# Attention in three passes, with maxima and exponentials of one pass side by side, scores by parts of the keys, and two row transfers in flight

## Chip, cores and metric

The kernel runs on one core of one Trainium2 chip, in one launch. The metric is the device time of the execution in microseconds (us); lower is better. A core has TensorE (PE; its weight loads are shown as PEld), VectorE (DVE), ScalarE (ACT), GpSimd (POOL) and SyncE (SP), which run side by side and wait for each other by semaphores. TensorE writes to PSUM, which has eight banks of 512 fp32 values per partition; SBUF is the working memory.

## What is computed

Two layers over 2048 tokens of width 128. Layer 0 is an attention block and a mixture of experts (eight experts, the two best per token); layer 1 is a recurrence over the tokens and a second mixture (one expert per token). The change lies in the attention of layer 0 and in the first sending of its tokens to the experts. The attention works on the first tokens only, in three iterations, and each may widen its window `cw` by a tenth:

```
def step(carry, i):
    qcur, prev, attn, cw, temp, done = carry
    ...
    scores = jnp.einsum('bhqd,bhkd->bhqk', sq, sk) * inv_sqrt_e
    in_win = pos < cw
    scores = jnp.where(in_win[None, None, None, :], scores, -jnp.inf)
    probs = jax.nn.softmax(scores, axis=-1)
    out = jnp.einsum('bhqk,bhkd->bhqd', probs, vp)
    iter_out = jnp.where(in_win[None, None, :, None], out, 0.0)
    diff = jnp.mean(jnp.abs(iter_out - prev))
```

There are 16 heads of width 8. The largest possible windows of the three iterations are 256, 281 and 309 keys (`WINDOWS`), so 2, 3 and 3 tiles of 128 tokens. These first three tiles of 128 tokens are the "near" tokens; the other 13 are the "far" tokens, which attention doesn't change.

## The kernel before

The program is written engine by engine, by hand: each engine runs its instructions in the order written, and semaphores join them.

**A pass of attention** (`attend(it)` on PE and on DVE, `softmax_exp(it)` on ACT; the text calls the iterations pass 0, 1 and 2). Queries and keys are split into bf16 pieces that are laid side by side in `stack`, 64 values a head, turned by TensorE (L1004, "turn", one for four heads), and copied to `qs` and `ks` (L765, L759). Even heads lie on the first 64 rows of the array, odd heads on the last 64 (`half`). Then come two halves of the pass:
- *Maxima.* For each head PE computes the scores with the queries on the partitions (L1028), nj matmuls of 256, 281 or 309 keys each in a bank of its own: banks 0 to 2 for even heads, 3 to 5 for odd ones. DVE takes the maximum over the keys (L1765) and frees the banks (`max_free`). After four heads DVE puts their maxima into `stack` (L1759), and PE turns the group again (`turn_maxima`), so that the maximum becomes a row of the queries and is subtracted by the matmul itself.
- *Exponentials.* For each head PE computes the scores again with the keys on the partitions (L1048, the "transposed scores"), ACT takes the exponential (L777, `probs_ready`), and PE weighs the values with them (L1053, `weigh_four`: four heads at once in 32-row strips of one bank, 6 or 7 by turns). ACT takes the sums out (`take`, L784), PE turns them back (`turn_out`, L1075), and DVE goes on from there (L1705) to the queries of the next pass or, after pass 2, to `attention_out`.

All 16 heads of maxima stand before the first transposed score; L1048 waits until `max_free` has come for the last heads.

**Around pass 1.** While pass 1 runs its exponentials, DVE picks the two experts of each far token (`choose`), PE counts the tokens of each expert (`count("far")`, L1184 and L1185, which in the order of PE stands after the transposed scores of head 7), and DVE reads the counts (L1580), plans the places of the sorted rows and works them out (`plan_far`, `place`), then the experts of the tiles and a few small things for layer 1 (up to L1836), and only then the queries of pass 2 (`next_queries(1)`, L1705).

**The far transfers.** When the places are there, POOL sends the 13 far tiles of rows twice, once per chosen expert, by indirect DMA (L585), from `token_rows` to the sorted rows in HBM. Before each it waits until the one before has landed; after 13 it writes the second set of place numbers (L543) first. SP waits for all 26 (`wait_scattered`) and then loads the first tiles of sorted rows (L380) for the experts.

**The experts** (`experts(0)`) start when these tiles, the scaled weights (`out_gated`) and, in the order of DVE, the output of attention and the normalisation of the near tokens are there: DVE runs `attention_out()` and `layernorm` of the near tiles before it takes the first tile of the experts (`bias_up`, L1910).

## Time and profile before

| | us |
|---|---|
| median of 3 runs | 455.07 (452.31 to 455.73) |
| the execution profiled | 457.89 |
| its span, first to last instruction | 456.2 |
| busy: PE / DVE / ACT / POOL | 305.5 / 302.1 / 171.8 / 173.6 |

The profile is of one execution. Times are from the start of its span; the span is cut into 40 equal slices of 11.4 us. "Busy" of PE counts instructions in flight, also when they are pipelined. The chain that ended last is 30% PE, 25% DVE, 20% DMA, 10% issue (time in which an engine waited for nothing that the profile shows). The heaviest piece of that chain by line is the far transfers with 15%. The passes of attention lie at about 38 to 71 us (pass 0), 83 to 128 (pass 1) and 141 to 188 (pass 2).

### The profile page before, as it was taken

Reading aid. Unit: us, or ns where it says so; the run is one execution under the profiler, and the core shown is the slowest. Engines: PE = TensorE matmul, PEld = TensorE weight load, DVE = VectorE, ACT = ScalarE, POOL = GpSimd, SP = SyncE. Lnnn points to the kernel's source line nnn. Section 1 sums busy time; section 2 is a strip of 40 time slices with the busy share of each in tenths; the row PEclk is TensorE's granted clock in tenths of the full one; section 3 lists DMA queues with packets and bytes.
Section 4 is the critical chain, followed back from the end, with each engine's and each line's share of the span. In section 5 each row is a group of like instructions: output and inputs, shape, how many; then the busy total and the mean of one; then the engine's idle time right before and its main releaser. Section 6 shows DMA issues by size and latency. Waiting matters only on the chain.

```text
span 456.2 us, 7413 instructions
## 1 busy us (share of the span) xinstructions
PE 305.5 (67%) x2070; PEld 221.0 (48%) x2071; DVE 302.1 (66%) x859; ACT 171.8 (38%) x331; POOL 173.6 (38%) x281
## 2 busy tenths in 40 slices
PE   2876886789926899697888999307716300689960
PEld 1662215333313332486887999303615300589960
DVE  7597976994779993278736565475888770377850
ACT  1144452217602167052425555647006600345520
POOL 9572870930233344302564455400000077044450
PEclk9986559555985558869889999856875555699995
DMA  2599700000000000031213221595000012323310
GB/s 77 105 368 361 206 3 0 1 1 1 13 18 29 23 25 25 24 54 54 56 51 71 63 65 37 154 282 166 1 1 1 0 63 105 94 70 74 94 50 0
DMA packets 37805, 32.93 MB, mean 72 GB/s; under 512 B 10765, under 2 KB 28770, under 8 KB 37776
## 3 DMA queue, kind: packets, MB, share of 16 engines
q1 hardware_dynamic: 33792, 25.10, 19.8%
q0 software_dynamic: 3936, 7.49, 5.2%
q8 instruction: 13, 0.21, 0.2%
q14 instruction: 16, 0.13, 0.1%
q10 hardware_dynamic: 48, 0.00, 0.0%
HBM read 19.50 MB, written 13.98 MB: 73 GB/s over the span
## 4 chain that ended last, share of the span: by engine, by line
PE 30%; DVE 25%; DMA 20%; issue 10%; ACT 5%; POOL 5%; SPq 2%; DVEq 1%; another core or an unknown queue 0%; POOLq 0%; ACTq 0%
DMA rows<-token_rows,posu 15%; PE ps L1237 9%; PE ps L1248 6%; POOL rows L585 4%; DVE mx L1765 3%; PE ps L1053 2%; PE ps L1028 2%; DVE stats L1373 2%; PE ps L1048 2%; DVE hb L1910 2%; SPq L293 1%; PE ps L1004 1%; DVE wide L2007 1%; PE ps L1205 1%; PE ps L1221 1%
## 5 line engine op out<-in xcount | busy, mean ns | idle before, releaser
L585 POOL DMA_INDIRECT rows<-token_rows,posu x48 | 51.9, 1080 | 147.1 <-DVE token_rows L1688 74.2
L1248 PE MATMUL ps<-w_out,hg 128*128 x496 | 67.2, 281 | 1.0 <-DVE ys L1921 0.7
L1910 DVE TENSOR_TENSOR hb<-ps,b_in 128x512 f32<-128x512 f32 x62 | 42.5, 686 | 36.2 <-PE ps L1237 31.3
L1248 PEld LDWEIGHTS ps<-w_out,hg 128*128 128x128 f32 x496 | 61.7, 196 | 1.8 <-issue 1.6
L597 POOL DMA_INDIRECT back<-ys,places x39 | 38.8, 995 | 52.0 <-DVE ys L1921 41.2
L866 ACT ACTIVATE hg<-hb 128x512 f32<-128x512 f32 x62 | 39.1, 630 | 41.4 <-DVE hb L1910 30.8
L1765 DVE TENSOR_REDUCE mx<-ps 128x2 f32<-128x512 f32 (+2 forms) x48 | 44.4, 949 | 5.4 <-PE ps L1028 5.1
L1237 PE MATMUL ps<-xsT,w_now 128*128 128x128 f32 x256 | 39.6, 304 | 10.1 <-issue 4.1
L1237 PEld LDWEIGHTS ps<-xsT,w_now 128*128 128x128 f32 x256 | 35.5, 214 | 12.3 <-issue 10.7
L1028 PE MATMUL ps<-feat,qs 64*128 64x281 bf16 (+2 forms) x128 | 33.3, 431 | 11.7 <-DVE mx L1765 7.3
L1221 PE MATMUL ps<-ident,xs 128*128 128x128 f32 x62 | 18.2, 297 | 32.5 <-DMA xs<-rows 32.2
L765 ACT COPY qs<-ps 128x768 bf16<-128x768 bf16 (+1 forms) x21 | 15.3, 728 | 63.8 <-PE ps L1004 63.8
L597 POOL DMA_INDIRECT out<-ys,rest x23 | 22.6, 984 | 34.3 <-DVE ys L1929 25.1
L1004 PE MATMUL ps<-identb,stack 128*128 128x128 bf16 x152 | 20.5, 310 | 18.7 <-DVE stack L1509 18.7
L1237 PE MATMUL ps<-xsT,qs 128*128 128x128 f32 x240 | 32.0, 277 | 1.0 <-DVE hb L1910 1.0
L1048 PE MATMUL ps<-qs,feat 64*128 64x281 bf16 (+2 forms) x128 | 29.4, 391 | 3.4 <-ACT wide L777 2.7
L1921 DVE TENSOR_TENSOR ys<-ps,b_out 128x128 f32<-128x128 f32 x62 | 17.8, 287 | 20.0 <-PE ps L1248 15.1
L1237 PEld LDWEIGHTS ps<-xsT,qs 128*128 128x128 f32 x240 | 29.5, 193 | 1.1 <-issue 1.1
L857 ACT ACTIVATE xsT<-ps,modcol 128x128 f32<-128x128 f32 x39 | 17.5, 452 | 31.6 <-PE ps L1221 26.0
L777 ACT ACTIVATE wide<-ps 128x512 f32<-128x512 f32 (+2 forms) x36 | 27.6, 812 | 4.3 <-PE ps L1048 4.0
L1004 PEld LDWEIGHTS ps<-identb,stack 128*128 128x128 bf16 x152 | 14.6, 141 | 27.4 <-DVE stack L1509 17.4
L1053 PE MATMUL ps<-wide,vpx 128*9 128x281 f32 (+2 forms) x192 | 27.3, 531 | 0.0
(388 smaller groups left out, 546.3 us busy)
## 6 DMA issues: line engine op xcount, KB each, us to landing
rows<-blank SPq DMA_DIRECT2D x20, 260.0 KB, 6.1
xs<-rows SPq DMA_DIRECT2D x62, 64.0 KB
w_in<-in_L_ffn_w_fc SPq DMA_DIRECT2D x1, 2048.0 KB, 13.7
w_in<-in_L_ffn_W SPq DMA_DIRECT2D x1, 2048.0 KB, 10.5
rest<-rows SPq DMA_DIRECT2D x23, 65.0 KB
token_rows<-in_L_attn_x SPq DMA_DIRECT2D x1, 832.0 KB, 8.4
wmod<-in_L_wmod SPq DMA_DIRECT2D x2, 384.0 KB, 4.5
rows<-token_rows,posu POOLq DMA_INDIRECT x48, 2.3
```

Of the source, the lines that this page charges most:

```text
L585: pool.indirect_dma_start(ROWS[l], bass.IndirectOffsetOnAxis(ap=posu[:, k, j:j + 1], axis=0), token_rows[:, j, 0:WIDTH[l]], None).then_inc ...
L597: pool.indirect_dma_start(where, bass.IndirectOffsetOnAxis(ap=target[r] if l else places[:, t, :].bitcast(U32)[:, 0:1], axis=0), ys[:, r, ...
L777: act.activation(probs[h % NPROBS][:, 0:nj, 0:nw], ps[:, 3 * b:3 * b + nj, 0:nw], ACT.Exp).then_inc(sem("probs_ready"), 1)
L866: act.activation(hg[:, c % RING, :], hb[:, c % 2, :], fn).then_inc(sem("hg_ready"), 1)
L1004: mm = pe.transpose(psb[:, bank, a * NATT + j * P:a * NATT + (j + 1) * P], stack[:, at:at + 2, :].rearrange("p h s -> p (h s)"), identb[:])
L1028: mm = pe.matmul(ps[:, 3 * b + j, 0:nw], half(qs, h)[:, j * P:(j + 1) * P], half(ks, h)[:, 0:nw], start=True, stop=True)
L1048: mm = pe.matmul(ps[:, 3 * b + j, 0:nw], half(ks, h)[:, j * P:(j + 1) * P], half(qs, h)[:, 0:nw], start=True, stop=True)
L1053: return pe.matmul(ps[OROW * q:OROW * q + HD + 1, 6 + g % 2, 0:nw], vpx[:, jk, h, :], probs[h % NPROBS][:, jk, 0:nw], start=(jk == 0), sto ...
L1237: mm = pe.matmul(ps[:, b, n * P:(n + 1) * P], w_ring[c % RING][:, n * P:(n + 1) * P], xsT[:, c % 2, :], start=True, stop=True)
L1248: mm = pe.matmul(ps[:, 6 + c % 2, 0:D], hg[:, c % RING, n * P:(n + 1) * P], w_out[:, bass.ds(e * NB + n, 1), :], start=(n == 0), stop=(n = ...
L1765: v.tensor_reduce(mx[:, 0:nj, h:h + 1], ps[:, 3 * b:3 * b + nj, 0:nw], AX.X, ALU.max).then_inc(sem("max_free"), 1)
L1910: v.tensor_tensor(hb[:, c % 2, :].rearrange("p (b t) -> p b t", b=NB), ps[:, c % RING if h_bank(l, t) is None else h_bank(l, t), :].rearra ...
```

## The change

- *One loop over the heads on PE.* Scores and maxima of heads 0 to 7 come first; then, for each h, the transposed scores of head h and the scores of head h + 8, with turns, weighings and turns of maxima between them.
- *Scores by parts of the keys.* `KEY_PARTS`: in pass 0 one part of 256 keys, in pass 1 parts of 170 and 111, in pass 2 of 170 and 139. A part is nj matmuls side by side in one bank, banks 0 and 1 by turns; DVE reduces each part by itself (`mx` has two of each), and `stack_maxima` takes the larger.
- *PSUM.* Banks 0 and 1 scores; 2 turns of maxima; 3 and 4 transposed scores of even heads, 5 and 6 of odd heads, written without gaps over the two banks (`exponents`), so that in passes 1 and 2 the matmul that meets the border is cut in two; 7 the weighed sums of all groups, so that each group waits for the `take` of the one before. The first four turns of a pass go to banks 3 to 6, ahead of the scores.
- *ACT.* The copies of the turned maxima (steps 4 to 7) stand between exponentials.
- *The count of the far experts* stands after the loop of the heads.
- *The far transfers.* Two semaphores by turns; each send waits for the one before the last.

```
+KEY_PARTS = [[(a, min(a + 512 // -(-n // P), n)) for a in range(0, n, 512 // -(-n // P))] for n in WINDOWS]
+MAXIMA0 = [HEADS * sum(len(p) for p in KEY_PARTS[:it]) for it in range(3)]
...
-        mx = sb("mx", [P, NA, HEADS])
+        mx = sb("mx", [P, 2, NA, HEADS])
...
+        TURN_AT = (3, 4, 5, 6, 2, 2, 2, 2)
+        def exponents(h, n):
+            b = 3 + 2 * (h % 2)
+            return ps[:, b:b + 2, :].rearrange("p a n -> p (a n)")[:, 0:n]
...
                 for j in range(NA, NT):
-                    if j > NA:
-                        pool.wait_ge(sem("scattered_far"), 16 * sent)
-                    send_row("far", 0, k, j)
+                    if sent > 1:
+                        pool.wait_ge(sem(("scattered_far", "scattered_odd")[sent % 2]), 16 * (sent // 2))
+                    send_row("far", 0, k, j, odd=bool(sent % 2))
                     sent += 1
...
-                exps(0, 2)
+                stack_copy(it, 4)
+                exps(0, 3)
+                stack_copy(it, 5)
+                exps(3, 7)
+                take(0)
+                stack_copy(it, 6)
+                exps(7, 11)
+                take(1)
                 stack_copy(it, 7)
-                exps(2, 8)
-                take(0)
-                exps(8, 12)
-                take(1)
-                exps(12, 16)
+                exps(11, 15)
                 take(2)
+                exps(15, 16)
                 take(3)
...
+                    parts = KEY_PARTS[it]
+                    for k, (lo, hi) in enumerate(parts):
+                        n = MAXIMA0[it] + len(parts) * h + k
+                        pe.wait_ge(sem("max_free"), n + 1)
                         for j in range(nj):
-                            mm = pe.matmul(ps[:, 3 * b + j, 0:nw], half(qs, h)[:, j * P:(j + 1) * P], half(ks, h)[:, 0:nw], start=True, stop=True)
+                            mm = pe.matmul(ps[:, n % 2, j * (hi - lo):(j + 1) * (hi - lo)], half(qs, h)[:, j * P:(j + 1) * P],
+                                           half(ks, h)[:, lo:hi], start=True, stop=True)
                         mm.then_inc(sem("s_ready"), 1)
...
                     if jk == 0:
-                        if g < 2:
-                            pe.wait_ge(sem("qs_act"), C0 + 6 + g)
-                        else:
-                            pe.wait_ge(sem("o_taken"), G0 + g - 1)
+                        if g:
+                            pe.wait_ge(sem("o_taken"), G0 + g)
...
+                for h in range(8):
+                    score(h)
+                    if h == 6:
+                        turn_maxima(0)
+                for h in range(HEADS):
+                    score_t(h)
+                    if h < 8:
+                        score(h + 8)
+                    if h % 4 == 2 and h < 11:
+                        turn_maxima(h // 4 + 1)
+                    g, k = divmod(h - 5, 4)
+                    if h >= 5 and k == 0:
+                        weigh_four(g, 0)
+                    elif h >= 5 and k == 1:
+                        weigh_four(g, 1)
+                        if nj == 3:
+                            weigh_four(g, 2)
                 if it == 1:
+                    count("far")
```

The order of the instructions on PE, in pass 1. Before the change, from head 7 of the exponentials to head 8 (L1048 transposed scores, L1053 weighing, L1184 and L1185 the count; an `x` says how many alike):

```order
L1048 MATMUL ps<-qs,feat 128x281 [waits probs_ready]
L1048 MATMUL ps<-qs,feat 128x281 x2
L1053 MATMUL ps<-wide,vpx 9x281 x4
L1184 MATMUL ps<-chosen,before 128x104 [waits chosen]
L1185 MATMUL ps<-chosen,onesb 128x104
L1048 MATMUL ps<-qs,feat 128x281 [waits qs_act,probs_ready]
L1048 MATMUL ps<-qs,feat 128x281 x2
```

The first rows are head 7, and the count stands between it and head 8. After the change, at head 2 of the exponentials (L1074 transposed scores, L1053 the scores of the maxima, now parts of 170 and 111 keys, L1020 the turn):

```order
L1074 MATMUL ps<-qs,feat 128x281 [waits probs_ready]
L1074 MATMUL ps<-qs,feat 128x231
L1074 MATMUL ps<-qs,feat 128x50
L1074 MATMUL ps<-qs,feat 128x281
L1053 MATMUL ps<-feat,qs 128x170 [waits max_free]
L1053 MATMUL ps<-feat,qs 128x170 x2
L1053 MATMUL ps<-feat,qs 128x111 [waits max_free]
L1053 MATMUL ps<-feat,qs 128x111 x2
L1020 MATMUL ps<-identb,stack 128x128 [waits qs_act,max_stack]
L1020 MATMUL ps<-identb,stack 128x128 x5
```

This is head 2 of the exponentials with head 10 of the maxima and a turn. Four matmuls stand where three stood for the transposed scores, six where three stood for the scores, and the turn comes between the heads. The end of pass 1 on PE after the change (L1201 and L1202 are the count, L1079 weighing, L1097 turning out):

```order
L1074 MATMUL ps<-qs,feat 128x281
L1201 MATMUL ps<-chosen,before 128x104 [waits chosen]
L1202 MATMUL ps<-chosen,onesb 128x104
L1079 MATMUL ps<-wide,vpx 9x281 [waits probs_ready,o_taken]
L1079 MATMUL ps<-wide,vpx 9x281 x2
L1079 MATMUL ps<-wide,vpx 9x281 [waits probs_ready]
L1079 MATMUL ps<-wide,vpx 9x281 x2
L1079 MATMUL ps<-hg,vpx 9x281 [waits probs_ready]
L1079 MATMUL ps<-hg,vpx 9x281 x2
L1097 MATMUL ps<-omap,wmod 128x68 [waits counts_read,o_taken,qs_act,max_free]
```

The count has moved from behind head 7 to behind the last transposed score of head 15. ACT in pass 2 after the change (L791 exponentials, L781 copies of turned maxima, L798 `take`):

```order
L781 COPY qs<-ps 128x768 [waits stackT]
L791 ACTIVATE wide<-ps 128x927 [waits st_ready] x3
L781 COPY qs<-ps 128x768 [waits stackT]
L791 ACTIVATE wide<-ps 128x927 [waits st_ready] x3
L791 ACTIVATE hg<-ps 128x927 [waits st_ready]
L798 COPY wmod<-ps 128x309 [waits oT_clear,weighed]
L781 COPY qs<-ps 128x768 [waits stackT]
L791 ACTIVATE hg<-ps 128x927 [waits st_ready]
L791 ACTIVATE wide<-ps 128x927 [waits st_ready,weighed] x3
L798 COPY wmod<-ps 128x309 [waits oT_clear,weighed]
L781 COPY qs<-ps 128x768 [waits stackT]
```

Before, three of these copies stood ahead of the first exponential, and the takes had no copy beside them.

## Rows read from the trace of the kernel before

**Rows 1.** The page, 40 slices: TensorE's granted clock in tenths.

```profile
PEclk9986559555985558869889999856875555699995
```

**Rows 2.** TensorE by stretches: us, busy (instructions), granted clock, DMA share, GB/s.

```profile
102.00:115.00 13.00, 12.41 (x75) 0.50 0.01 1
116.00:128.00 12.00, 11.89 (x103) 1.00 0.05 13
```

**Rows 3.** Timeline, far transfers (POOL, SP queue); start us, us, engine, line, operation [idle before].

```profile
120.27 1.13 POOL L585 DMA_INDIRECT rows<-token_rows,posu  x1 [25.46 <-DVE posu L1662]
...
190.34 0.97 POOL L585 DMA_INDIRECT rows<-token_rows,posu  x1 [1.58 <-DMA rows<-token_rows,posu]
192.85 1.75 SPq L380 DMA_DIRECT2D xs<-rows  x4
...
377.23 0.96 POOL L585 DMA_INDIRECT rows<-token_rows,posu  x1 [0.30 <-issue]
```

**Rows 4.** Timeline, VectorE from the outputs of pass 2 to the experts' tiles.

```profile
188.08 0.21 DVE L1705 TENSOR_SCALAR den<-ps 128x48 f32<-128x48 f32 x1 [11.91 <-PE ps L1075]
...
198.57 0.68 DVE L1910 TENSOR_TENSOR hb<-ps,b_in 128x512 f32<-128x512 f32 x1
...
201.78 0.69 DVE L1910 TENSOR_TENSOR hb<-ps,b_in 128x512 f32<-128x512 f32 x1 [0.75 <-PE ps L1237]
```

**Rows 5.** Timeline, maxima of pass 0 on PE and DVE.

```profile
39.37 2.68 DVE L1765 TENSOR_REDUCE mx<-ps 128x2 f32<-128x512 f32 x4 [0.79 <-PE ps L1028]
40.12 1.20 PE L1028 MATMUL ps<-feat,qs 64*128 64x256 bf16 x4 [0.28 <-DVE mx L1765]
...
44.94 0.92 PE L1028 MATMUL ps<-feat,qs 64*128 64x256 bf16 x4
45.58 0.69 DVE L1765 TENSOR_REDUCE mx<-ps 128x2 f32<-128x512 f32 x1 [0.39 <-PE ps L1028]
```

**Rows 6.** Timeline, maxima of passes 1 and 2 on PE and DVE.

```profile
84.92 4.00 DVE L1765 TENSOR_REDUCE mx<-ps 128x3 f32<-128x843 f32 x4
...
142.59 4.33 DVE L1765 TENSOR_REDUCE mx<-ps 128x3 f32<-128x927 f32 x4
...
150.60 0.82 PE L1004 MATMUL ps<-identb,stack 128*128 128x128 bf16 x6
151.35 1.49 PE L1028 MATMUL ps<-feat,qs 64*128 64x309 bf16 x6
152.34 1.12 DVE L1765 TENSOR_REDUCE mx<-ps 128x3 f32<-128x927 f32 x1 [0.51 <-PE ps L1028]
...
157.26 1.12 DVE L1765 TENSOR_REDUCE mx<-ps 128x3 f32<-128x927 f32 x1 [0.51 <-PE ps L1028]
```

**Rows 7.** Timeline, PE in the exponentials: transposed scores (L1048) and weighing (L1053).

```profile
57.49 0.61 PE L1048 MATMUL ps<-qs,feat 64*128 64x256 bf16 x4
...
113.08 0.90 PE L1048 MATMUL ps<-qs,feat 64*128 64x281 bf16 x6
...
169.29 1.22 PE L1053 MATMUL ps<-wide,vpx 128*9 128x309 f32 x8
170.44 0.95 PE L1048 MATMUL ps<-qs,feat 64*128 64x309 bf16 x3
...
172.47 0.96 PE L1048 MATMUL ps<-qs,feat 64*128 64x309 bf16 x6
```

**Rows 8.** Timeline, the count of pass 1, the last head, VectorE behind it.

```profile
112.79 0.27 PE L1184 MATMUL ps<-chosen,before 128*128 128x104 bf16 x1
...
113.25 0.27 DVE L1580 COPY pose<-ps 128x104 f32<-128x104 f32 x1 [5.90 <-PE ps L1185]
...
119.91 0.53 PE L1048 MATMUL ps<-qs,feat 64*128 64x281 bf16 x3
...
123.61 0.28 DVE L1836 TENSOR_TENSOR woy<-woy,modrow 128x128 f32<-128x128 f32 x1
...
128.00 0.21 DVE L1705 TENSOR_SCALAR den<-ps 128x48 f32<-128x48 f32 x1 [4.10 <-PE ps L1075]
```

More of the change, by code:

```diff
@@ L410, in wait_scattered @@
                     lo, hi, experts = GROUPS[g]
-                    sp.wait_ge(sem("scattered_" + g), 16 * (hi - lo) * experts)
+                    n = (hi - lo) * experts
+                    if g == "far":
+                        sp.wait_ge(sem("scattered_odd"), 16 * (n // 2))
+                        n -= n // 2
+                    sp.wait_ge(sem("scattered_" + g), 16 * n)
                 def wait_sent(tiles):
@@ L1009, in _ @@
             for g in range(4):
[L1010 removed]
+                turn_group(g, (0, 1, 2, 6)[g], NA, "kstackT")
             def attend(it):
@@ L1034, in turn_maxima @@
                     pe.wait_ge(sem("max_stack"), G0 + g + 1)
-                    turn(g)
-                def scores_t(lo, hi):
-                    for h in range(lo, hi):
-                        b = h % 2
-                        if h < 2:
-                            pe.wait_ge(sem("max_free"), H0 + HEADS + 1 + h)
-                        else:
-                            pe.wait_ge(sem("probs_ready"), H0 + h - 1)
-                        if h % 4 == 0:
-                            pe.wait_ge(sem("qs_act"), C0 + 4 + h // 4)
-                        for j in range(nj):
-                            mm = pe.matmul(ps[:, 3 * b + j, 0:nw], half(ks, h)[:, j * P:(j + 1) * P], half(qs, h)[:, 0:nw], start=True, stop=True)
-                        mm.then_inc(sem("st_ready"), 1)
+                    pe.wait_ge(sem("qs_act"), C0 + 3 + g)
@@ new lines, in turn_maxima, with score_t @@
+                    turn(4 + g)
+                def score_t(h):
+                    if h >= 2:
+                        pe.wait_ge(sem("probs_ready"), H0 + h - 1)
+                    if h % 4 == 0:
+                        pe.wait_ge(sem("qs_act"), C0 + 4 + h // 4)
+                    e = exponents(h, 1024)
+                    for j in range(nj):
+                        a = j * nw
+                        cuts = [a, a + nw] if a // 512 == (a + nw - 1) // 512 else [a, 512, a + nw]
+                        for lo, hi in zip(cuts, cuts[1:]):
+                            mm = pe.matmul(e[:, lo:hi], half(ks, h)[:, j * P:(j + 1) * P], half(qs, h)[:, lo - a:hi - a], start=True, stop=True)
+                    mm.then_inc(sem("st_ready"), 1)
@@ L1079, in attend @@
                 pe.wait_ge(sem("q_stack"), it + 1)
+                if it == 0:
+                    pe.wait_ge(sem("ks_act"), 4)
                 turn(0)
+                turn(1)
                 if it:
                     pe.wait_ge(sem("asum"), it)
-                    pe.matmul(ps[:, 3, 0:1], ones[:], asum[:], start=True, stop=True).then_inc(sem("change"), 1)
-                turn(1)
-                pe.wait_ge(sem("qs_first"), it + 1)
-                if it == 0:
-                    pe.wait_ge(sem("values"), 1)
-                    pe.wait_ge(sem("ks_act"), 4)
-                else:
-                    pe.wait_ge(sem("ks_set"), 2 * it - 1)
@@ L1107, in attend @@
-                scores(12, 16)
-                turn_maxima(2, 4)
-                scores_t(0, 2)
-                turn_maxima(3, 5)
-                scores_t(2, 6)
-                for g in range(3):
-                    weigh_four(g, 0)
-                    scores_t(4 * g + 6, 4 * g + 7)
-                    weigh_four(g, 1)
-                    scores_t(4 * g + 7, 4 * g + 8)
-                    if nj == 3:
-                        weigh_four(g, 2)
-                    if it == 1 and g == 0:
-                        count("far")
-                    if g < 2:
-                        scores_t(4 * g + 8, 4 * g + 10)
@@ L1125, in attend @@
-                pe.wait_ge(sem("o_taken"), G0 + 2)
+                    if it == 1:
+                        pe.wait_ge(sem("lg_read"), 1)
+                        pe.wait_ge(sem("ks_masked"), 2)
+                    pe.matmul(ps[:, 7, 0:1], ones[:], asum[:], start=True, stop=True).then_inc(sem("change"), 1)
+                else:
+                    pe.wait_ge(sem("values"), 1)
+                turn(2)
+                turn(3)
+                for h in range(8):
+                    score(h)
+                    if h == 6:
+                        turn_maxima(0)
```

99 lines of the change are left out of this document (47 added, 52 removed).

## Prediction

> **What bounds the kernel now.** I read the page first: the clock line [rows 1] shows TensorE at half speed in most of slices 3 to 16, which are the three attention passes. Then the granted clock by stretch [rows 2]: in pass 1 the maxima and, up to 115 us, the exponentials run at 0.50 (1.2 GHz), the rest at 1.00 (2.4 GHz). Of these 13 us from 102 to 115 TensorE is busy 12.4, so the clock stays low although it hardly rests. Pass 2 does the same by the clock line. Then the timeline of each pass, for what the two halves cost. Last the chain of waits, which says DMA from 120 to 193 us: 26 row transfers of the far tokens, one at a time, the last issued at 190.34, and the first tile of the experts is loaded at 192.85 [rows 3]. But this is a near tie: pass 2 hands over its outputs at 188.08 and VectorE works on them until 198.57, when it can take the first tile of the experts [rows 4]. So two chains end within 2 us of each other: the transfers, and the passes.
>
> The execution profiled took 457.89 us, 1.7 more than its span and 2.8 above the median of 455.07. The sum is made against its rows, and its result is added to the median.
>
> **The transfers.** Each takes some 2.55 us from one to the next and keeps POOL busy for 0.97. Where nothing is waited for, in the second layer, the next one starts 1.27 after the last [rows 3]. With two in flight the period lies between 1.27 and 2.55; I take 1.4, near the first, since transfers do overlap there: 26 x 1.4 and 3 us at the pause in the middle is 39 instead of 72.5 us. They will start later (below, at 128), and end near 167, well ahead of pass 2. Worth: the transfers leave the chain. TensorE's first tile then waits only for the passes. VectorE is next: its work from 188.08 to 198.57 doesn't shrink, and behind it its waits for TensorE in the first tiles (0.75 before the third tile [rows 4]) shrink. TensorE's lead would be 1.4 us or so, since its first tile waited for the load until 1.9 after 192.85; I take -1.4, and the bounds are 0 and -2.
>
> **Heads 0 to 7 of a pass: scores and maxima alone.** Now a head has two parts in passes 1 and 2, 170 keys and 111 or 139, each in one bank. From the start of the matmuls to the reduction, 512 columns took 0.64 (44.94 to 45.58), and 927 columns 0.99 [rows 5, 6]; the release of a bank 0.08 (0.67 after 39.37 the reduction ends, 40.12 the matmuls start). A reduction takes 0.67 for 512 elements, 1.00 for 843, 1.08 for 927 (quarters of the fours), so about 0.67 for the first part, 0.49 or 0.58 for the second. The second part is shorter than what a first part needs on TensorE, so the cycle is 0.67 + 0.08 + 0.64 = 1.4 us a head, against 1.00 or 1.08 (1.23 with the turn that stands between four heads now, 4.92 from 152.34 to 157.26). Here the halves cost more than they give. From the first reduction to the first transposed score: 7 x 1.4 and 0.6 for the last part, the turn of the first maxima and its copy: 10.4.
>
> **Heads 0 to 7 of the exponentials beside heads 8 to 15 of the maxima.** Even and odd heads use different halves of the rows: six matmuls of two heads take 0.96, three of one head 0.95 [rows 7]. So a transposed score (0.77) of one head hides beside the maxima's cycle, and the cycle stays 1.4. What needs the whole array is added: a turn 0.76 (150.60 to 151.35), a weighing of four heads 1.15 (169.29 to 170.44) in pass 2, 1.05 in pass 1. When one is put in, the next score waits for it, for the transposed score on its own half, and for its own 0.64: 0.2 + x + 0.77 + 0.64 - 1.4. With x = 0.76 (after head 2) 1.0; x = 1.15 (head 5) 1.4; x = 0.76 + 2.3 (head 6) 3.3. Sum of pass 2: 8 x 1.4 + 5.7 = 16.9, of pass 1: 11.2 + 5.2 = 16.4. So the transposed scores of head 8 start 27.3 (26.8) after the first reduction. Before they start at 172.47 and 113.08, after reductions at 142.59 and 84.92: 29.9 (28.2). Gain: 2.6 in pass 2, 1.4 in pass 1. Far less than half of a maxima phase, because at 1.2 GHz the matmuls were no small thing beside the reductions.
>
> **The last eight heads and the tail.** They are as before but for: a turn and a copy (0.8) moved in among them; one bank for the outputs where there were two, so that ScalarE's take of a group stands between two exponentials and waits for TensorE's weighing. I add 1.7, from 0.8 + 0.76 and small waits; bounds 0 and 5. The tail has three groups turned out behind the last but one wait where there were two, and the take before it: +0.4. The turns and weighings behind head 6 stand in one row (3.1 us of full array); TensorE was given its full clock before after such rows, so I let it come a microsecond or two earlier: -0.5. Pass 2 in all: -2.6 + 1.7 + 0.4 - 0.5 = -1.0.
>
> **Pass 1 has a second chain.** The count of the far experts stood behind head 7's weighing (112.79); it now stands behind the transposed scores of head 15, because all the heads are one loop. VectorE waits for it at 113.25 and then has 10.6 us of planning and placing (to 123.89), ahead of the next queries in its queue; it then waited 4.10 for TensorE, to 128.00 [rows 8]. Head 15 was at 119.91. Now it is at 119.91 + 0.45 (the change matmul stands behind a second turn) - 1.4 + 1.7 - 0.5 = 120.2, and VectorE is done 0.5 (the scores) + 0.46 (counts) + 10.6 later: 131.8. TensorE's own end would be near 128.5. The cover of 4.10 is gone, and pass 2 starts 3.8 later. The transfers, which need the places, start at 128 instead of 120.27.
>
> **Pass 0.** One part a head, and the reductions set the pace at 0.67 to 0.7 as now. Two turns moved ahead of head 0 cost 1.0, the first heads take 7 x 0.67 and 0.6 for the end, the overlapped ones 8 x 0.72 and 3.5 for what is put in (by the rule above with matmuls of 256): head 8 is reached 15.6 after 39.37, at 55.0, where it is 57.5 now [rows 7]. The last heads give 1.8 of the 2.5 back. I take -0.6; bounds -1.5 and +1.
>
> **Sum:** pass 0 -0.6, pass 1 +3.8, pass 2 -1.0, experts -1.4: +0.8, which is 458.7 in this execution and 455.9 on the median.
>
> **Rivals.**
> A. The full clock comes early in each overlapped stretch. For it: TensorE has two streams to draw on and no waits there. Against: 12.41 of 13 us busy at 0.50 [rows 2]. At 2.4 GHz the cycle is the two reductions, 1.25, and what is put in costs half: 12.3 instead of 16.9, in both passes, and 1 in pass 0: 9.5 less, 446.4. The Trainium skill (TensorE: Matmul & The Clock Gate, section Why this matters for your kernels) says that keeping TensorE busy without gaps gets it to the full clock; by that rule this case would be the likeliest, and this trace doesn't bear it out between 102 and 115 us.
> B. The last eight heads run in lockstep. One output bank (weighing waits for the take, the take for the weighing, exponentials queued behind the take on ScalarE) and the copies: 5 us a pass instead of 1.7 in passes 1 and 2, 1 more in pass 0, part of it under the late VectorE in pass 1: about +5, 461. It decides from 18.5 us between head 8's transposed scores and the end of pass 2 (15.6 now). For it: ScalarE's order has four such places a pass. Against: TensorE has other work ready at most of them.
> C. The full clock doesn't come before the end of a pass. The 12 us from 116 to 128 at full clock [rows 2] would be some 17 (not 24, since exponentials of 0.9 set part of the pace): +10 over two passes, 466.
> D. The change doesn't do what it says: two transfers don't overlap, and the period stays 2.55. From 128 they end at 128 + 66.3 + 0.6 = 195, 2 later than now, and the load follows: 457.5.
>
> **How the numbers follow.** Forecast 0.47, with its own range 452 to 460; A 0.25 (in part or full); B 0.18; C 0.07; D 0.03. A measurement of this kernel tells about 1% (4.6 us) from no change. Faster by over that: A, 0.25. Slower: B, C and a little of the forecast's edge, 0.27. Within: 0.48. The range reaches half into A and to B: 448.5 to 461.5.
>
> **What would show it.** Right: reductions of 0.67 and 0.5 with waits on TensorE between them, clock 0.50 until about head 7 of the exponentials; in pass 1 VectorE arrives at the queries after TensorE, with no wait; rows of transfers 1.3 to 1.5 apart, done some 20 us before the experts; the first tile waits for the outputs of pass 2. Wrong: a clock of 1.00 within 5 us of the first transposed score (A), or waits of ScalarE for weighings over 3 us a pass (B).

## The result: slower by 1.7%

| | us |
|---|---|
| before, median of 4 runs | 453.78 (452.31 to 455.73) |
| after, median of 4 runs | 461.66 (460.64 to 463.20) |
| ratio | 1.0174, 95% interval 1.0115 to 1.0233 |
| execution profiled after | 460.87, its span 459.1 |

The forecast was 455.9 in 448.5 to 461.5, with "within 1%" the likeliest; the result lies 0.2 above the range. The ratios of this document leave out executions that took over 1.5% more than the fastest of the same kernel. The time of the execution profiled before, 457.89, is above all four runs here, so the two spans (456.2 and 459.1) understate the difference, and what follows compares stretches, not ends.

The page's clock line after the change, which answers to [rows 1]:

```profile
PEclk9885595556875558979899999857765555699995
```

The half-speed slices are where they were. TensorE by stretches. The columns are the length in us; what PE, PEld, DVE, ACT and POOL were busy, with instructions; the granted clock, the DMA share and GB/s. First come the two streams side by side in pass 2 and what follows, then the same of pass 1:

```profile
157.21:177.22 20.01, 16.89 (x116) 8.97 (x117) 9.94 (x19) 8.56 (x11) 6.50 (x7) 0.54 0.20 41
177.22:194.83 17.61, 15.79 (x134) 7.77 (x134) 13.63 (x25) 9.80 (x13) 0.00 (x0) 1.00 0.01 1
94.23:110.40 16.17, 15.50 (x116) 9.09 (x117) 8.68 (x19) 8.16 (x11) 0.00 (x0) 0.50 0.01 2
110.40:128.57 18.17, 16.63 (x139) 8.27 (x136) 11.69 (x48) 9.19 (x13) 0.42 (x1) 0.90 0.00 1
```

The stretch from the first transposed score to that of head 8 took 16.17 in pass 1 (forecast 16.4) but 20.01 in pass 2 (forecast 16.9), and TensorE was busy in 16.89 of these. It stood idle for 3.1 us there, and for 0.7 in pass 1. The fourth row has a clock of 0.90: in pass 1 the full clock came at 110.66, and from 117.49 to 120.90 the granted clock was 0.50 again. Pass 1 on VectorE and PE, answering to [rows 6 to 8] (L1053 is now the scores of the maxima, L1074 the transposed scores):

```profile
83.95 1.10 DVE L1789 TENSOR_REDUCE mx<-ps 128x3 f32<-128x510 f32 x2
85.33 1.10 DVE L1789 TENSOR_REDUCE mx<-ps 128x3 f32<-128x510 f32 x2 [0.28 <-PE ps L1053]
...
94.23 0.88 PE L1074 MATMUL ps<-qs,feat 64*128 64x281 bf16 x4
...
120.69 0.27 PE L1201 MATMUL ps<-chosen,before 128*128 128x104 bf16 x1
...
121.14 0.27 DVE L1597 COPY pose<-ps 128x104 f32<-128x104 f32 x1 [5.01 <-PE ps L1202]
...
131.72 0.21 DVE L1722 TENSOR_SCALAR den<-ps 128x48 f32<-128x48 f32 x1
```

A head's two reductions repeat every 1.38 us. VectorE waits 5.01 for the late count, and reads the outputs of pass 1 at 131.72 with no wait ahead: it comes after TensorE now. Then pass 2, on ScalarE, VectorE, PE and SP's queue:

```profile
146.59 1.50 ACT L781 COPY qs<-ps 128x768 bf16<-128x768 bf16 x2 [3.49 <-remote]
146.79 1.19 DVE L1789 TENSOR_REDUCE mx<-ps 128x3 f32<-128x510 f32 x2 [0.43 <-PE ps L1053]
...
161.73 0.82 PE L1020 MATMUL ps<-identb,stack 128*128 128x128 bf16 x6
163.48 1.03 PE L1053 MATMUL ps<-feat,qs 64*128 64x170 bf16 x6
165.58 0.80 ACT L781 COPY qs<-ps 128x768 bf16<-128x768 bf16 x1 [3.34 <-remote]
166.52 0.93 PE L1074 MATMUL ps<-qs,feat 64*128 64x309 bf16 x4 [2.02 <-ACT qs L781]
167.01 1.78 ACT L791 ACTIVATE wide<-ps 128x927 f32<-128x927 f32 x2 [0.64 <-remote]
167.06 1.19 DVE L1789 TENSOR_REDUCE mx<-ps 128x3 f32<-128x510 f32 x2 [3.15 <-remote]
167.12 1.75 SPq L391 DMA_DIRECT2D xs<-rows  x4
...
194.83 0.21 DVE L1722 TENSOR_SCALAR den<-ps 128x48 f32<-128x48 f32 x1 [2.19 <-PE ps L1097]
```

Read the middle rows together. The turn at 161.73 ends at 162.55, but ScalarE copies it only at 165.58. The scores at 163.48 end at 164.51, but VectorE takes their maximum only at 167.06. Neither engine had other work, and the view names no instruction that released them ("remote"). SP, which waits for the last of the 26 transfers, starts its load at 167.12: ScalarE's exponential, VectorE and SP go on within 0.11 us of each other. The row at 146.59 is a smaller one of the kind: the turn before it ended at 144.36, and the copy starts as the thirteenth transfer has landed (POOL goes on at 146.68). Call this a hold-up.

The transfers themselves did what the change says: issued 128.15 to 164.79, mostly 1.3 apart, and out of the chain of waits (its DMA share fell from 20% to 5%). The experts then start as forecast, answering to [rows 4]:

```profile
205.16 0.68 DVE L1935 TENSOR_TENSOR hb<-ps,b_in 128x512 f32<-128x512 f32 x1
...
207.26 0.69 DVE L1935 TENSOR_TENSOR hb<-ps,b_in 128x512 f32<-128x512 f32 x1 [0.15 <-PE ps L1254]
```

The third tile stands 12.4 after the outputs of pass 2, where it stood 13.7 in the profile shown of the kernel before (and 12.5 in a second profile of it, before_again below).

### The profile page after: what moved, and what is told of

Read it like the earlier page. It is cut to its first block, busy times and chain, and to the rows that moved or that the text cites. A ratio compares the mean times of both kernels' runs of the same rounds, so it can differ in the third digit from the quotient of the medians.

```text
span 459.1 us, 7709 instructions
## 1 busy us (share of the span) xinstructions
PE 304.9 (66%) x2198; PEld 237.0 (52%) x2199; DVE 306.3 (67%) x891; ACT 173.4 (38%) x331; POOL 170.5 (37%) x281
## 4 chain that ended last, share of the span: by engine, by line
PE 36%; DVE 29%; issue 13%; ACT 6%; DMA 5%; POOL 4%; SPq 3%; another core or an unknown queue 1%; DVEq 1%; POOLq 0%; ACTq 0%
PE ps L1254 7%; PE ps L1265 6%; PE ps L1053 6%; PE ps L1079 4%; DVE mx L1789 4%; POOL rows L600 4%; PE ps L1074 3%; PE ps L1020 2%; DVE stats L1390 2%; SPq L297 1%; PE ps L1175 1%; DMA xs<-rows 1%; DVE wide L2032 1%; PE ps L1222 1%
## 5 line engine op out<-in xcount | busy, mean ns | idle before, releaser
L600 POOL DMA_INDIRECT rows<-token_rows,posu x48 | 49.3, 1028 | 122.5 <-DVE token_rows L1705 71.7
L1789 DVE TENSOR_REDUCE mx<-ps 128x3 f32<-128x510 f32 (+1 forms) x80 | 48.0, 631 | 28.7 <-PE ps L1053 24.4
L1053 PE MATMUL ps<-feat,qs 64*128 64x170 bf16 (+3 forms) x224 | 38.8, 330 | 11.2 <-DVE mx L1789 9.9
L1254 PEld LDWEIGHTS ps<-xsT,w_now 128*128 128x128 f32 x256 | 35.1, 213 | 10.4 <-issue 8.5
L1053 PEld LDWEIGHTS ps<-feat,qs 64*128 64x128 bf16 x224 | 21.4, 125 | 27.1 <-DVE mx L1789 18.1
L1074 PE MATMUL ps<-qs,feat 64*128 64x309 bf16 (+6 forms) x160 | 31.4, 327 | 5.9 <-ACT qs L781 4.9
L781 ACT COPY qs<-ps 128x768 bf16<-128x768 bf16 (+1 forms) x21 | 15.0, 730 | 49.2 <-PE ps L1020 42.3
L1946 DVE TENSOR_TENSOR ys<-ps,b_out 128x128 f32<-128x128 f32 x62 | 17.9, 289 | 21.3 <-PE ps L1265 17.6
L791 ACT ACTIVATE wide<-ps 128x512 f32<-128x512 f32 (+2 forms) x36 | 28.0, 806 | 8.7 <-PE ps L1074 6.4
L1020 PE MATMUL ps<-identb,stack 128*128 128x128 bf16 x152 | 17.8, 289 | 18.9 <-DVE stack L1526 17.0
L873 ACT ACTIVATE xsT<-ps,modcol 128x128 f32<-128x128 f32 x39 | 17.6, 455 | 28.9 <-PE ps L1238 24.0
L1238 PEld LDWEIGHTS ps<-ident,xs 128*128 128x128 f32 x62 | 9.5, 154 | 33.5 <-issue 31.0
```

What stands on the lines that cost most here:

```text
L600: pool.indirect_dma_start(ROWS[l], bass.IndirectOffsetOnAxis(ap=posu[:, k, j:j + 1], axis=0), token_rows[:, j, 0:WIDTH[l]], None).then_inc ...
L791: act.activation(probs[h % NPROBS][:, 0:nj, 0:nw], exponents(h, nj * nw).rearrange("p (j n) -> p j n", j=nj), ACT.Exp).then_inc(sem("probs ...
L1020: mm = pe.transpose(psb[:, bank, a * NATT + j * P:a * NATT + (j + 1) * P], stack[:, at:at + 2, :].rearrange("p h s -> p (h s)"), identb[:])
L1053: mm = pe.matmul(ps[:, n % 2, j * (hi - lo):(j + 1) * (hi - lo)], half(qs, h)[:, j * P:(j + 1) * P], half(ks, h)[:, lo:hi], start=True, st ...
L1074: mm = pe.matmul(e[:, lo:hi], half(ks, h)[:, j * P:(j + 1) * P], half(qs, h)[:, lo - a:hi - a], start=True, stop=True)
L1238: pe.transpose(ps[:, 4 + c % 2, 0:P], xs[:, c % RING, :], ident[:]).then_inc(sem("xs_used"), 1)
```

## The experiments

Thirteen runs were made beside the two profiles above. What was read off each trace is collected first; the columns are, in us, P1: first maximum of pass 1 to VectorE's reading of its outputs; gap: from there to the first maximum of pass 2; P2/8: first maximum of pass 2 to the transposed scores of head 8; P2: to VectorE's reading of the outputs; E: from there to its first tile of the experts; last: issue of the last far transfer; then the ratio to the kernel before on the same chip, with its interval.

| run | P1 | gap | P2/8 | P2 | E | last | ratio |
|---|---|---|---|---|---|---|---|
| before (profile shown) | 43.1 | 14.6 | 29.9 | 45.5 | 10.5 | 190.3 | 1 |
| before_again | 42.4 | 14.7 | 30.0 | 45.6 | 10.2 | 190.3 | one run |
| before_two | 43.3 | 14.6 | 31.7 | 46.9 | 9.7 | 155.9 | 1.0036 (0.9989 to 1.0084) |
| before_mixed | 42.9 | 14.5 | 29.9 | 45.3 | 10.7 | 177.1 | 0.9973 (0.9930 to 1.0017) |
| after | 47.8 | 15.1 | 30.4 | 48.0 | 10.3 | 164.8 | 1.0174 (1.0115 to 1.0233) |
| after_again | 46.3 | 15.3 | 32.7 | 51.9 | 10.3 | 164.9 | 1.0200 (1.0148 to 1.0253) |
| after_one | 46.0 | 14.7 | 27.5 | 45.1 | 14.5 | 199.4 | 1.0151 (1.0100 to 1.0201) |
| apart | 55.1 | 15.1 | 34.5 | 51.8 | 10.0 | 176.3 | 1.0418 (1.0339 to 1.0498) |
| count_early | 43.1 | 15.1 | 30.7 | 48.3 | 10.3 | 162.7 | 1.0052 (1.0015 to 1.0089) |
| early_one | 42.9 | 14.6 | 27.5 | 45.1 | 14.7 | 193.3 | 1.0087 (1.0050 to 1.0124) |
| early_one_turn | 42.8 | 14.7 | 27.5 | 44.6 | 13.2 | 192.1 | 1.0079 (1.0043 to 1.0114) |
| early_two_turn | 42.4 | 15.0 | 30.9 | 48.1 | 10.3 | 158.9 | 1.0035 (1.0001 to 1.0068) |
| early_mixed | 42.8 | 15.4 | 27.5 | 44.6 | 10.3 | 176.6 | 1.0000 (0.9962 to 1.0038) |
| early_mixed_b | 45.4 | 14.5 | 27.5 | 47.6 | 10.3 | 175.8 | 0.9960 (0.9926 to 0.9994) |
| late_pairs | 45.4 | 14.5 | 27.1 | 45.3 | 9.7 | 180.1 | one run |

**1. Does it repeat?** after_again is the changed kernel:

> The changed kernel once more, with a profile. In its first trace pass 2 holds a stall of 3.0 us at 163 to 166 in which ScalarE and VectorE both wait for TensorE's signals long after its matmuls ended (ScalarE's copy of the turned maxima 3.3 after the end of what it did before, VectorE's next maximum 3.15). Theory M (the stall is a chance event of one execution): it is gone here or stands elsewhere, the transposed scores of head 8 start 27 to 28 us after the first maximum of pass 2 (30.4 in the first trace), and the time still is 459 to 463. Theory S (the stall belongs to this program): it stands at the same place again, 2 to 3.5 us long.

The hold-ups were there again (ratio 1.0200): ScalarE's second copy of pass 2 came after 3.50 of idleness that no instruction explains, and three waits of 1.95 to 2.25 stood at 164 to 167; head 8 came at 32.7. So theory S, but for the exact place. The pass took 51.9 in all; 1.6 of that isn't a hold-up: from head 8 on it took 19.2 where it took 17.6 after the change, and the granted clock was 0.50 from 187.45 to 190.86. before_again is the kernel before:

> The kernel before once more, for a second profile. Its first profiled execution took 457.89 us, 4.1 above the median of its plain runs, and VectorE and ScalarE have waits of 2.4 us in the experts that no work explains. Theory M: here they are gone or elsewhere, and the execution takes 452 to 456. Theory S: the same waits at the same places. The passes of attention should repeat within 0.5 us under both: first maximum of pass 1 to VectorE's reading of its outputs 43.1, of pass 2 45.5.

It took 454.28, and its passes repeated within 0.7 (P1, where 0.5 was expected) and 0.1 (P2). It has unexplained waits too, of 2.5 and 3.1 us, but all of them in the experts, none in the passes.

**2. The count.**

> After the change, with the count of the far experts put behind the transposed scores of head 12 in place of head 15 (nothing else is moved). Theory P (the late count costs pass 1 its cover): VectorE reads the counts at about 116 in place of 121.1, is done with planning 4.7 earlier, at 127.0, then waits for TensorE's outputs of pass 1 (128.6); pass 2 starts 3.1 earlier, and the time falls by 3 us, to 458.5. Rival (what VectorE does late is absorbed before the experts start): the time stays within 1 us.

```
                 for h in range(HEADS):
                     ...
+                    if it == 1 and h == 12:
+                        count("far")
-                if it == 1:
-                    count("far")
```

VectorE's reading of the count and of the outputs of pass 1, in count_early:

```profile
118.87 0.27 DVE L1597 COPY pose<-ps 128x104 f32<-128x104 f32 x1 [0.41 <-PE ps L1202]
...
129.62 0.21 DVE L1722 TENSOR_SCALAR den<-ps 128x48 f32<-128x48 f32 x1 [0.21 <-DVE woy L1861]
```

From the first maximum (86.47 here) that is 32.4 for the count against 37.2 after the change, 4.8 earlier, and 43.1 for the outputs against 47.8 and 46.3: 3.1 to 4.6 gained, of which 3.1 was expected. Pass 1 is then as long as before the change. The ratio fell from 1.0200 to 1.0052 on the same chip, 6.8 us, more than this term; 3.6 of it is that pass 2 was 51.9 in the one profile and 48.3 in the other (2.0 of that in the first eight heads, 1.6 the clock behind them). Between after_one and early_one below, which differ in the same edit and ran on one chip, it is 2.9 us.

**3. Pairs of transfers in the kernel before.**

> The kernel before, with two far transfers in flight and nothing else of the change. Theory P: the transfers end 27 to 30 us earlier (period 1.3 to 1.5 against 2.55; first tile's load near 160 in place of 192.85), and the experts' first tiles then wait for pass 2 alone: -1.4 us, between 0 and -2. Rival (the denser transfers slow what runs beside them): pass 2 gets longer by 1 us or more, and the time doesn't fall.

The edit is the change's own for `send_row`, `wait_scattered` and POOL's loop. VectorE, PE, SP and ScalarE in pass 2 of before_two:

```profile
153.09 1.13 DVE L1770 TENSOR_REDUCE mx<-ps 128x3 f32<-128x927 f32 x1 [2.05 <-PE ps L1033]
154.28 2.05 PE L1033 MATMUL ps<-feat,qs 64*128 64x309 bf16 x6 [2.23 <-issue]
...
158.11 2.15 DVE L1770 TENSOR_REDUCE mx<-ps 128x3 f32<-128x927 f32 x2 [1.72 <-PE ps L1033]
158.21 1.75 SPq L380 DMA_DIRECT2D xs<-rows  x4
158.87 0.80 ACT L770 COPY qs<-ps 128x768 bf16<-128x768 bf16 x1 [7.10 <-remote]
```

VectorE goes on at 158.11 and SP's load follows at 158.21, when the last transfer has landed. P2 is 1.4 longer, E 0.5 to 0.8 shorter: the rival. The gain of leaving the chain is paid back, and the time doesn't fall clear of its interval.

**4. One in flight again.**

> The changed kernel with one far transfer in flight again (each send waits for the one before it); everything else as after the change. In the traces with two in flight, pass 2 has waits of VectorE and ScalarE for TensorE that last 1.3 to 3.5 us beyond TensorE's matmuls and end in the same tenth of a microsecond as a landing of a far transfer. Theory F (two transfers in flight beside a pass hold up TensorE's signals): these waits are gone; in pass 2 the transposed scores of head 8 start 26.8 to 27.8 after the first maximum (30.4 and 32.7 with two in flight), ScalarE's second copy of the pass starts within 0.3 of the end of its turn, and although the transfers now end near 195 the time falls by 3 to 4.5 us. Rival G (the stalls come from the new order of the passes itself): they stay, the transfers end near 197 and the time rises by 0 to 3.

```
-                    if sent > 1:
-                        pool.wait_ge(sem(("scattered_far", "scattered_odd")[sent % 2]), 16 * (sent // 2))
+                    if j > NA:
+                        pool.wait_ge(sem(("scattered_odd", "scattered_far")[sent % 2]), 16 * ((sent + 1) // 2))
```

Head 8 at 27.5 (the prediction had 27.3) and the gap back at 14.7: the hold-ups are gone from the passes. But the time came only to 1.0151, which its interval doesn't tell from the 1.0174 and 1.0200 with pairs, since the transfers, begun at 129 because of the late count, now end so late that the experts wait. POOL, SP's queue, PE and VectorE in after_one:

```profile
199.44 0.97 POOL L600 DMA_INDIRECT rows<-token_rows,posu  x1 [1.59 <-DMA rows<-token_rows,posu]
201.75 1.75 SPq L391 DMA_DIRECT2D xs<-rows  x4
203.61 0.98 PE L1238 MATMUL ps<-ident,xs 128*128 128x128 f32 x2 [5.84 <-DMA xs<-rows]
206.83 0.69 DVE L1935 TENSOR_TENSOR hb<-ps,b_in 128x512 f32<-128x512 f32 x1 [4.08 <-PE ps L1254]
```

This is what my expectation left out: E is 14.5 in place of 10.3. With the earlier count (both edits together) E stays so:

> The changed kernel with the count behind head 12 and one far transfer in flight. Theory P and F together: 3 less from the earlier count and 3 to 4.5 less from the signals; about 457 where the change gives 463 to 464, and within 1% of the kernel before, 0 to 0.5% above or below it. Transfers from 126 to 193; the experts' first tile then no longer waits for them.

And with the last turn moved, on PE and on ScalarE:

> As the one before it, and the last turn of maxima moved from behind head 10 to behind head 9 of the exponentials, with ScalarE's copy ahead of head 10's exponential. In each pass TensorE waited 0.8 us for this copy at head 12. Theory: that wait goes, 0.5 to 0.8 a pass, 1.5 to 2 us in all (pass 0 may give nothing, since VectorE's own work ends it). Rival: the copy delays the exponentials of heads 10 and 11 by as much, and nothing is gained.

```
-                    if h % 4 == 2 and h < 11:
+                    if h in (2, 6):
                         turn_maxima(h // 4 + 1)
...
                     if h >= 5 and k == 0:
                         weigh_four(g, 0)
+                        if h == 9:
+                            turn_maxima(3)
...
-                exps(7, 11)
-                take(1)
+                exps(7, 10)
                 stack_copy(it, 7)
+                exps(10, 11)
+                take(1)
```

In early_one E is 14.7, so it comes to 1.0087 and not to 1.000 to 1.005. Moving the last turn took 0.5 from P2 (the part from head 8 on went from 17.6 to 17.1), as expected per pass, but in the whole time the two can't be told apart.

**5. Overlap against no overlap.**

> The changed kernel with maxima and exponentials apart: all 16 heads of scores first, then the 16 transposed scores, with the parts of the keys, the PSUM layout, the late count and the two transfers in flight kept; ScalarE's copies of the turned maxima stand ahead of the exponentials. Theory P (a head in parts costs 1.4 us, a transposed score hides wholly beside it): the first transposed score of pass 2 comes 15 x 1.4 + 0.6 and some 2 for the turns, so 23.5 to 24.5, after the first maximum (18.6 before the change), and head 8's 11 later: 34.5 to 35.5 against 27.3; so 7.5 us a pass more than after the change in passes 1 and 2, +15 to +17 in all. Rival (side by side the two streams slow each other, so that little is hidden): +5 to +8.

```
-                for h in range(8):
+                for h in range(HEADS):
                     score(h)
-                    if h == 6:
-                        turn_maxima(0)
+                    if h in (6, 10, 14):
+                        turn_maxima(h // 4 - 1)
                 for h in range(HEADS):
                     score_t(h)
-                    if h < 8:
-                        score(h + 8)
-                    if h % 4 == 2 and h < 11:
-                        turn_maxima(h // 4 + 1)
+                    if h == 1:
+                        turn_maxima(3)
...
```

(ScalarE's copies of the first three groups stand ahead of the exponentials, the fourth behind the second of them.) The first transposed score of pass 2 comes 23.7 after the first maximum (18.6 before the change), head 8 34.5. That seems to be 5.1 for the parts of the keys, and 7.0 for doing the streams side by side (34.5 to 27.5). But this pass has pairs beside it, and a hold-up. The second parts of heads 3, 7 and 11 on VectorE, and SP's queue:

```profile
164.60 1.89 DVE L1787 TENSOR_REDUCE mx<-ps 128x3 f32<-128x417 f32 x3
...
170.55 1.89 DVE L1787 TENSOR_REDUCE mx<-ps 128x3 f32<-128x417 f32 x3
...
178.62 3.08 DVE L1787 TENSOR_REDUCE mx<-ps 128x3 f32<-128x417 f32 x5 [0.60 <-PE ps L1053]
178.62 1.75 SPq L391 DMA_DIRECT2D xs<-rows  x4
```

Four heads took 5.95, the next four 8.07, and these end as the last transfer has landed: 2.1 us of hold-up. Without it the parts cost 3.0 in pass 2, and side by side gives 4.9. In pass 1, which has no transfers beside it, the same differences are 3.8 (17.4 to 21.2) and 5.0 (31.4 to 26.4). So side by side is worth 5 us in either pass, not the 7.5 of theory P, and not as little as the rival wants. The whole came to 2.2 to 2.4% more than the change, 10 to 11 us, below the 15 to 17 expected and above the rival's 5 to 8: twice 5 us.

**6. Where the pairs stand.** early_mixed is early_one_turn with pairs in the first 13 transfers, between the passes, and one in flight in the last 13:

```
-                    if j > NA:
+                    if k == 0 and sent > 1:
+                        pool.wait_ge(sem(("scattered_far", "scattered_odd")[sent % 2]), 16 * (sent // 2))
+                    if k and j > NA:
                         pool.wait_ge(sem(("scattered_odd", "scattered_far")[sent % 2]), 16 * ((sent + 1) // 2))
```

> The changed kernel with the count behind head 12, the last turn of maxima moved, and the far transfers two in flight in the first 13 (which run between the passes) but one in flight in the last 13 (beside pass 2). Theory F: 13 x 1.33, a pause of 2 and 13 x 2.55, so the last is issued near 175 (192 with one in flight throughout) and the experts' first tile doesn't wait: VectorE's first tile 10.0 us after it has read the outputs of pass 2 (13.1 with one in flight throughout); head 8 of the exponentials stays 27.5 after the first maximum. So 3 us less than with one in flight throughout, 0 to 0.3% above the kernel before. Rival (the time isn't set by these waits): no gain.

> The kernel before with the far transfers two in flight in the first 13 and one in flight in the last 13; nothing else. Theory F: pass 2 as in the kernel before (first maximum to the outputs 45.5; 46.9 with two in flight throughout), transfers end near 172, the load leaves the chain, VectorE's first tile 9.4 after the outputs in place of 10.0: 0.5 to 1.5 us less than the kernel before, about what can just be measured. Rival: pass 2 is held up all the same, and the time stays.

> As early_mixed, but the first 13 transfers one at a time and the last 13 two in flight. Theory F: the last 13 run from about 158 to 175, beside the second half of pass 2; waits of VectorE or ScalarE for TensorE that end with a landing, 1.5 to 3.5 us long, stand near the last of them, at 170 to 176, and not at 141 to 146 or at 160 to 164. Rival (the hold-up belongs to a place in pass 2, whatever the transfers do): it stands at the transposed scores of head 3 or 4 again, some 20 us after the pass began.

early_mixed met its numbers: last transfer 176.6, E 10.3, P2/8 27.5, ratio 1.0000. That is 0.8%, 3.6 us, below one in flight throughout (on another chip). It isn't free of hold-ups: ScalarE's second copy of pass 2 comes at 142.03 after 3.51 of idleness, its turn having ended at 139.56, when the thirteenth transfer has landed, and the gap is 15.4. before_mixed is 0.27% below the kernel before, which its interval doesn't tell from nothing; its E is 10.7 where 9.4 was expected, so its profile shows no gain either. late_pairs contradicts half of what I expected: VectorE has one wait for which the profile names no releaser, of 0.71 us at 169.18, and none of 1.5 to 3.5 near the last transfers (issued up to 180). It does have a hold-up, a small one: the transposed scores at 165.60 end at 166.55 and ScalarE takes them at 167.73; the scores at 166.35 end at 167.33, and VectorE takes their second part at 169.18. The maximum that follows is 0.8 later in the pass than in early_mixed_b (23.7 after the first maximum against 22.9); head 8 is early all the same, since here the full clock came at 169.28, 25 us after the first maximum. So pairs are needed for a long hold-up in a pass, but don't always bring one. The deciding pair of runs differs in the last 13 transfers alone, on one chip:

> As early_mixed, but two far transfers in flight throughout; beside early_mixed_b this differs in one thing, whether the last 13 transfers, beside pass 2, go in pairs. Theory F: pass 2 is held up again, first maximum to head 8 of the exponentials 30 to 33 (27.5 in early_mixed), and the time is 3 to 4 us above early_mixed_b. Rival (the hold-up was something of those executions, and late_pairs, which had it only at 1 us, is the rule): less than 1.5 us above.

> early_mixed once more, for the comparison on one chip: 27.5 from the first maximum of pass 2 to head 8 of the exponentials, VectorE's first tile 10.0 after it has read the outputs, and the time within 0.4% of the kernel before.

ScalarE, VectorE and SP's queue in early_two_turn, then ScalarE and VectorE at the same copy and the same maximum in early_mixed_b:

```profile
161.21 0.80 ACT L781 COPY qs<-ps 128x768 bf16<-128x768 bf16 x1 [3.34 <-remote]
161.22 1.75 SPq L391 DMA_DIRECT2D xs<-rows  x4
161.32 1.19 DVE L1792 TENSOR_REDUCE mx<-ps 128x3 f32<-128x510 f32 x2 [2.35 <-remote]
```

```profile
159.73 0.80 ACT L783 COPY qs<-ps 128x768 bf16<-128x768 bf16 x1 [0.68 <-PE ps L1023]
...
161.04 1.19 DVE L1794 TENSOR_REDUCE mx<-ps 128x3 f32<-128x510 f32 x2 [1.29 <-PE ps L1056]
```

early_mixed, run in two sets of 12, came to 1.0000 and 0.9960: the new passes with the count early and the transfers mixed are level with the kernel before or just below it. P2/8 is 30.9 in early_two_turn against 27.5, 3.4 more, and the ratios 1.0035 and 0.9960 differ by 0.0075, 3.4 us; their intervals don't meet. But the medians of all twelve executions of each are 457.20 and 454.99, which is 2.2 us. Theory F holds in what it says of the pass, and in time the last 13 pairs cost 2.2 to 3.4 us. Read P2 of these two profiles with care: it is 48.1 and 47.6, for in early_mixed_b the full clock came 35 us after the first maximum, in early_two_turn 29, so that the part from head 8 on took 20.1 and 17.1. The long hold-ups stand in all four traces of the side-by-side passes with pairs up to the last transfer beside pass 2 (30.4 to 32.7), a shorter one each in apart and before_two, and none in the first eight heads of the five with one in flight there (27.5); late_pairs (27.1) has the small one.

## Why the prediction was wrong

- *The timing of the two streams: right.* The cycle of a head was forecast at 1.4 and is 1.38; the first transposed score 10.4 after the first maximum is 10.3 in pass 1 and 10.4 in pass 2; head 8 in pass 1 was forecast at 26.8 and came at 26.4. The clock stayed at 0.50 all through this stretch of pass 1 with TensorE busy 15.50 of 16.17, so rival A fell. (In pass 2 the side-by-side stretch took 17.1 with one in flight, forecast 16.9.) The Trainium skill (TensorE: Matmul & The Clock Gate, Why this matters for your kernels), by which keeping TensorE busy gets it to the full clock, is not borne out by this stretch either.
- *The count in pass 1: right in kind and near in size.* Forecast: VectorE done at 131.8, 3.8 late. The measured 131.72 meets it partly by luck: the pass began 0.97 earlier than before (83.95), and from 117.49 to 120.90 the clock was at 0.50, which I hadn't foreseen. From its first maximum the pass took 47.8, and 46.3 in after_again, where the forecast amounts to 46.9 (131.8 - 84.92). That is 3.2 to 4.7 longer than before; count_early took 3.1 to 4.6 of it back. In time the edit gave 2.9 us in the one comparison on one chip and 6.8 in the other.
- *Pass 0: right in sum by luck.* Outputs were read 1.0 earlier (70.44 against 71.41; forecast 0.6), but after_again, with the same instructions, read them at 72.95, 1.0 later than before_again (71.95). After the change the full clock came at 59.46, in after_again not before 112. In the first profile TensorE had ended 2 us before VectorE's reading: since its maxima end later, VectorE came late from its own work on the tokens. I hadn't looked at what VectorE does behind the maxima of pass 0.
- *The last eight heads: nearly right.* Forecast 1.7 + 0.4 - 0.5 on 15.6, so 17.2; pass 2 took 17.6 in four of the profiles. B's sign, 18.5, was passed in two, after_again (19.2) and early_mixed_b (20.1), and there it was the clock, at 0.50 for longer: nearer to rival C. B's 461 meets the result, but not by B's lockstep.
- *The transfers: the step that failed.* "The transfers leave the chain ... I take -1.4": they did leave it, and the experts' third tile came 1.3 sooner after the outputs (13.7 to 12.4), though only 0.1 sooner than in before_again (12.5). What I costed at nothing was the effect of denser transfers on the engines beside them. It was 0.5 at the start of pass 2 and 2.9 in its first eight heads (30.4 against 27.5 with one in flight): 3.4 in the profile, 5.9 in that of after_again, and 2.2 to 3.4 us in the time where the last 13 were isolated. So the edit costs 2 us or more in the profile, where I had -1.4 (before_two, the edit alone, came to +1.6 us, with zero inside its interval), and no rival of mine had it; D asked only whether transfers overlap each other.
- *The sum.* Forecast -0.6 + 3.8 - 1.0 - 1.4 = +0.8. Up to the third tile of the experts the profiles show 207.26 - 201.78 = +5.5, and the second ones (after_again, before_again) 212.38 - 200.69 = +11.7; the medians differ by 7.9, which lies between. The hold-ups are 3.4 of the first and 5.9 of the second. Without them 2.1 is left of the first, against 0.8: pass 1 has 0.9 more than forecast and the last eight heads 0.4, pass 0 0.4 less. Of the second 5.8 is left: pass 0 is 1.0 longer, pass 1 3.9, the last eight heads 3.5, the first eight 2.4 shorter, and the experts give nothing. So with the hold-ups costed the forecast would have been near the first profile and still short of the second; much of what is left goes with the full clock, which comes at another moment in each execution. From the first tile of the experts to the end of the span the fifteen traces take 254 to 258 us with no order by kernel.

What the hold-up is stays open. Shown: TensorE's matmuls had ended, the engines that wait for them go on when a transfer lands, in the passes it needs pairs of GpSimd's transfers, and late_pairs shows that pairs aren't enough for a long one. The semaphores' records in the trace after the change, which no view prints, say where it sits: the turn that ended at 162.54 raised its semaphore at 165.56, and the scores that ended at 164.08 and 164.51 theirs at 167.04 and 167.09, where a turn that ended at 156.32 did so at 156.34. So TensorE's signals themselves came 2.6 to 3.0 us late, and ScalarE and VectorE answered at once. One more thing is in the traces: with one in flight all 416 completion records of the 26 transfers are there, with pairs throughout only 207 to 243. The signals' records go missing too: between the issues of the fourteenth and the last transfer TensorE, VectorE and ScalarE gave 92 signals in after_one, all recorded, and 59 after the change, with 37 records. In the experts of the kernel before, where some records are missing as well (289 for 358 signals from 200 to 300 us), there are unexplained waits too, of 2.39 us at 266.9. So the recording may have a part in it. The Trainium skill (NOTIFIC — the notification-queue block, 7.1 Overflow: three behaviours, one of which stalls the engine) says that the block which writes such records holds back those who feed it rather than lose one inside. No run here shows that: records are missing here all the same, and as there is a span and a clock for each timed run, each seems to have been recorded, and none was timed without.

## What to carry to other kernels

A transfer that leaves the chain isn't free: ask what runs beside it when it gets denser, and put the dense part where the busy engines rest (13 transfers in pairs between two passes and 13 single ones beside pass 2 brought 2.2 to 3.6 us over either pure form). When loops are merged, look at every instruction that stood between them: the count moved back by eight heads cost more than the merging gained, and at head 12 it leaves pass 1 as long as it was. Splitting a reduction into parts to free a bank is paid in handshakes, 3 to 4 us a pass here, so the overlap that it buys (5 us here) must be worth more. And take two profiles of either kernel: to the third tile of the experts one pair of them differed by 5.5 us and the other by 11.7.

## Not expected of the hardware

- Pairs of indirect transfers from GpSimd follow each other mostly every 1.27 to 1.4 us (one by one up to 3.3), single ones mostly every 2.55 to 2.7 (up to 4.65).
- ScalarE and VectorE can go on 2 to 3.8 us after the TensorE work that they wait for has ended, at the landing of a transfer that they don't wait for, in the trace (early_two_turn: the turn at 156.60 ends at 157.42, the copy starts at 161.21).
- The full clock comes at another moment of the pass in each execution: with the same instructions it came at 110.60 and at 117.81, and pass 1 took 42.8 and 45.4 (early_mixed and early_mixed_b).
